# Attention over sorted edges: the destination rows held 23 times in DRAM

## The chip, the cores and the metric

The kernel runs on one core of one Trainium2 chip. The metric is the device time of one execution, in microseconds; smaller is better. TensorE (PE, with its weight loads shown apart as PEld), VectorE (DVE), ScalarE (ACT), GpSimd (POOL) and the DMA queue of SyncE (SPq) each run their own list of instructions in order and wait for one another by semaphores. DMA transfers of all queues run on the core's 16 DMA engines.

## The reference

Two graph layers over 12,500 nodes of 256 channels and 200,000 edges that are sorted by `dst`. The first is a weighted sum of neighbours. The second, where the change lies, is an attention in which node `c` attends to the sources `r` of its edges, with 8 heads of 32 channels:

```python
h = jnp.maximum(_layernorm(x, axis=-1), 0.0)
x = x + _L0_gnn_ref(h, L0_gnn_weight, edge_weight, src, dst)
h = jnp.maximum(_layernorm(x, axis=-1), 0.0)
# _L1_gnn_ref(h, edges): q, k, v = h @ W.T + b, in 8 heads; r = src, c = dst
qe = q[:, c, :]
ke = k[:, r, :]
ve = v[:, r, :]
sim = jnp.einsum('hed,hed->eh', qe, ke) * scale
m = jax.ops.segment_max(sim, c, num_segments=bs)
p = jnp.exp(sim - m[c])
s = jax.ops.segment_sum(p, c, num_segments=bs)
attn = p / s[c]
out_e = attn.T[..., None] * ve
agg = jax.ops.segment_sum(out_e, c, num_segments=bs)
return agg @ Wo.T + bo
```

## The kernel before

The program is a row of blocks that end in a barrier of all engines: the first layer (to about 3,290 us), the projections to q, k and v (to about 3,704 us), the **edge tables** (3,704 to 3,785 us), the **attention loop** (3,785 to about 6,942 us) and the output product (to 7,142 us).

**Edge tables.** 128 edges make a column, and a column that meets two blocks of 128 nodes stands once for each. There are 110 windows of 16 columns (`NW2`, `W2`), rounded up to 14 chunks of 128 columns (`C2` = 14, `R2` = 1792). For each chunk `c`, POOL gathers `fg` (src, dst and more of 128 columns), DVE forms `dlf`, the node number of each edge inside its block, ACT narrows it to bf16 as `dlb` (two buffers, `t_narrow`) and makes `brk` (marks where dst changes, two buffers), and SP stores both: `drows` (L1177) and `breaks` (L1180). ACT may write `dlb` for chunk `c` only when the store of chunk `c - 2` has landed, and likewise `brk`. ACT also copies a row `ends` (L1242). After the last chunk DVE works alone on rows made of `ends` (L1309 to L1339), and then the barrier falls. SP ends its list by waiting for the last two stores of each kind.

`drows` is one row in DRAM of `R2 * P` = 229,376 bf16 values: the node numbers of all columns, one after another.

**Attention loop.** It runs over 440 steps of 4 columns, 4 steps to a window. In a window every engine needs a one-hot matrix `OT` of 128 nodes x 16 columns x 128 edges. SP loads it as numbers: all 128 partitions get the same 16 x 128 = 2048 values (4 KB) of `drows`, 512 KB in one DMA (L1434), into one of three buffers, two windows ahead of use. DVE compares each partition with its own number (L1732), which makes the one-hot matrix. PE multiplies it with `qb`, the queries of the block (L1508, `expand`), DVE multiplies by the gathered keys and adds up per head (L1667, L1676), a chain over PE, DVE and ACT finds running maxima (L1535 to L1577, L1752 to L1799, L1628 to L1651), ACT takes the exponential and weighs the values (L1622, L1610, with a share for DVE, L1688), PE sums them per node (L1525) and DVE adds them to `acc` (L1713). POOL gathers keys and values, one indirect DMA of 128 rows of 2,080 bytes for every column (L1484), up to 11 steps ahead. SP also loads `qb` (L1412), stores finished blocks of `acc` (L1426) and loads `nf` from `breaks` (L1442). The order of all of this is written out by hand, step by step, in each engine's list.

The load, in the kernel before:

```python
e.dma_start(OT[:, w % 3, :, :].rearrange("p j e -> p (j e)"),
            drows[0:1, w * W2 * P:(w + 1) * W2 * P].to_broadcast([P, W2 * P])).then_inc(
    dls.sem(w), 16)
```

Of the kernel before, what the change touches and what calls it, by code (L numbers as in the profile page):

```python
# [7 lines left out]
P = 128  # L8
# [19 lines left out]
W2 = 16  # L28
NW2 = -(-2 * (T2 + NB - 1) // W2)
J2 = NW2 * W2  # L30
C2 = -(-J2 // P)
R2 = C2 * P
PH = NH * (W2 + 1)
BIG = 1.0e30
SCALE = float(np.float32(1.0) / np.sqrt(np.float32(32.0)))

# [3 lines left out]
BF16 = mybir.dt.bfloat16  # L40
# [50 lines left out]
def build(nc, x, src, dst, edge_weight, weight, Wq, bq, Wk, bk, Wv, bv, Wo, bo, out):  # L91
    def dram(name, shape, dt=F32):
        return nc.dram_tensor(name, shape, dt, kind="Internal").ap()

    fields = dram("fields", (JP, 3 * P))
    breaks = dram("breaks", (R2, P + 1))
    drows = dram("drows", (1, R2 * P), BF16)
    accd = dram("accd", ((NB + 1) * P, NH * 33))
    srows = dram("srows", (1, JP * P))
    sums = [dram(f"sums{k}", (NB * P + P, D)) for k in range(NS)]  # L100
# [8 lines left out]
    with ExitStack() as top:  # L109
# [3 lines left out]
        def S(name):  # L113

            if name not in known:
                known[name] = nc.alloc_semaphore(name)
            return known[name]
# [7 lines left out]
        def sb(stack, name, shape, dt=F32):  # L125
            return stack.enter_context(nc.sbuf_tensor(name, shape, dt))
# [4 lines left out]
        hw = [Landing(nc.alloc_semaphore(f"landed{i}")) for i in range(26)]  # L131
# [41 lines left out]
        with ExitStack() as stack:  # L173
# [9 lines left out]
            @block.sync  # L183
            def _(e):
                e.dma_start(da[:, :], dst.rearrange("(p e) -> p e", e=1600)).then_inc(loaded.sem(0), 16)
                e.wait_ge(S("st_fill"), 1)
                e.dma_start(db[0:124, :], dst[1:1 + 124 * 1600].rearrange("(p e) -> p e", e=1600)).then_inc(
                    loaded.sem(1), 16)
                e.dma_start(db[124:125, 0:1599], dst[1 + 124 * 1600:E].rearrange("(p e) -> p e", e=1599)).then_inc(
                    loaded.sem(2), 16)  # L190
                e.wait_ge(S("st_pad"), 3)
                edge_loads(e, src, ints[:, 0, :, :], edges[0].sem(0))
# [946 lines left out]
        with ExitStack() as stack:  # L1139
# [22 lines left out]
            bb = sb(stack, "bb", [P, R2 // 2 + 1])  # L1162
            bi = sb(stack, "bi", [P, R2 // 2], I32)
            keys, frows = Ring(hw[0:1], 2), Ring(sw[0:NF])
            dput, bput = Ring(hw[1:3]), Ring(hw[3:5])
            block = stack.enter_context(nc.Block())

            @block.sync
            def _(e):
                e.wait_ge(S("t_fill"), 1)  # L1170
                e.dma_start(kf[:, 0:6].rearrange("p (c a) -> p c a", a=1), fields[0:12 * P, P:P + 1].rearrange(
                    "(c p i) f -> p c i f", p=P, i=2)[:, :, 0, :]).then_inc(keys.sem(0), 16)
                e.dma_start(kf[0:64, 6:7], fields[12 * P:JP, P:P + 1].rearrange("(p i) f -> p i f", i=2)[:, 0, :]).then_inc(
                    keys.sem(1), 16)
                for c in range(C2):
                    e.wait_ge(S("t_narrow"), c + 1)
                    e.dma_start(drows[0:1, c * P * P:(c + 1) * P * P].rearrange("a (p f) -> (a p) f", f=P),  # L1177
                                dlb[:, c % 2, :]).then_inc(dput.sem(c), 16)
                    e.wait_ge(S("t_brk"), c + 1)
                    e.dma_start(breaks[c * P:(c + 1) * P, :], brk[:, c % 2, :]).then_inc(bput.sem(c), 16)  # L1180
                for c in range(C2 - 2, C2):
                    e.wait_ge(dput.sem(c), dput.value(c))
                    e.wait_ge(bput.sem(c), bput.value(c))

            @block.gpsimd
# [43 lines left out]
            def _(e):  # L1229
                e.wait_ge(S("t_fill"), 2)  # L1230
                for c in range(C2):
# [5 lines left out]
                    if c >= 2:  # L1237
                        e.wait_ge(bput.sem(c), bput.value(c - 2))
                    e.activation(brk[:, c % 2, 1:P], dif[:, c % 2, 0:P - 1], ACT.Copy, scale=-BIG).then_inc(
                        S("t_brk"), 1)  # L1240
# [101 lines left out]
        frows.over(C2)  # L1342
        dput.over(C2)
        bput.over(C2)


        with ExitStack() as stack:
# [12 lines left out]
            ab = sb(stack, "ab", [1, 2, NH, W2 + 1])  # L1360
            tops = sb(stack, "tops", [1, 2 * PH + 2])
            runs = sb(stack, "runs", [1, 2, PH])
            sides = sb(stack, "sides", [1, 2, NH, W2])
# [8 lines left out]
            dls, nfs, flushed = Ring(hw[8:11]), Ring(hw[11:14]), Ring(hw[14:22])  # L1372
            hs = tops[:, 0:PH]
            ts = tops[:, PH:2 * PH]
            block = stack.enter_context(nc.Block())
# [18 lines left out]
            @block.sync  # L1394
            def _(e):
                blocks, slots, news = registers(e, "l1s"), registers(e, "l1t"), registers(e, "l1u")
                fslot, fend, fblk = registers(e, "l1v"), registers(e, "l1w"), registers(e, "l1x")

                def queries(h):

                    if 4 * h >= NJ:
                        return
                    e.load(blocks[:4], irow[0:1, 4 * h:4 * h + 4])
                    own = [e.snap(r, min_val=0, max_val=NB - 1) for r in blocks[:4]]
                    e.load(slots[:4], irow[96:97, 4 * h:4 * h + 4])
                    slot = [e.snap(r, min_val=0, max_val=NQ - 1) for r in slots[:4]]
                    e.load(news[:4], irow[64:65, 4 * h:4 * h + 4])
                    new = [e.snap(r, min_val=0, max_val=1) for r in news[:4]]
                    for j in range(4 * h, 4 * h + 4):
                        if j >= NQ:  # L1410
                            e.wait_ge(S("l_expanded"), (j - NQ) // 2 + 1)
                        e.dma_start(qb[:, bass.ds(slot[j % 4], 1), :].rearrange("p a d -> p (a d)"),  # L1412
                                    qt[bass.ds(own[j % 4] * P, P), :], cond=new[j % 4],
                                    bounds_check="skip_entire_dma").then_inc(qs.sem(j), 16)

                def flush(h):

                    e.load(fslot[:4], irow[96:97, 4 * h:4 * h + 4])
                    slot = [e.snap(r, min_val=0, max_val=RB - 1) for r in fslot[:4]]
                    e.load(fend[:4], jrow[0:1, 4 * h:4 * h + 4])  # L1420
                    end = [e.snap(r, min_val=0, max_val=1) for r in fend[:4]]
                    e.load(fblk[:4], jrow[32:33, 4 * h:4 * h + 4])
                    own = [e.snap(r, min_val=0, max_val=NB) for r in fblk[:4]]
                    for j in range(4 * h, 4 * h + 4):
                        e.wait_ge(S("l_add"), j + 1)
                        e.dma_start(accd[bass.ds(own[j % 4] * P, P), :],  # L1426
                                    acc[:, bass.ds(slot[j % 4], 1), :].rearrange("p a d -> p (a d)"),
                                    cond=end[j % 4], bounds_check="skip_entire_dma").then_inc(flushed.sem(j), 16)

                def rows(w):  # L1430
                    if w < NW2:
                        if w >= 3:
                            e.wait_ge(S("l_expanded"), 4 * (w - 3) + 4)
                        e.dma_start(OT[:, w % 3, :, :].rearrange("p j e -> p (j e)"),  # L1434
                                    drows[0:1, w * W2 * P:(w + 1) * W2 * P].to_broadcast([P, W2 * P])).then_inc(
                            dls.sem(w), 16)

                def limits(w):
                    if w < NW2:
                        if w >= 3:  # L1440
                            e.wait_ge(S("l_bw2"), w - 2)
                        e.dma_start(nf[:, w % 3, :], breaks[w * W2:(w + 1) * W2, :].rearrange(  # L1442
                            "(a j) f -> a j f", a=1).to_broadcast([NH, W2, P + 1])).then_inc(nfs.sem(w), 16)

                rows(0)
                queries(0)
                rows(1)
                limits(0)
                for p in range(STEPS + 1):
                    w, u = p // 4, p % 4  # L1450
                    if u % 2 == 0:
                        queries(p // 2 + 1)
                    if u == 1:
                        rows(w + 2)
                    if u == 3:
                        limits(w + 1)
                    if u % 2 == 0 and 10 <= p < NQD + 10:
                        flush((p - 10) // 2)
                for j in range(NJ - RB, NJ):
                    e.wait_ge(flushed.sem(j), flushed.value(j))  # L1460
# [136 lines left out]
            def _(e):  # L1597
# [16 lines left out]
                for p in range(STEPS):  # L1614
# [10 lines left out]
                    if u == 1 and on:  # L1625
                        if v:
# [4 lines left out]
                        e.wait_ge(S("l_tops"), v + 1)  # L1631
                        e.copy(tops[:, :].rearrange("a (i x) -> a i x", i=2)[:, :, 0:PH].rearrange(  # L1632
                            "a i (h k) -> a i h k", h=NH)[:, :, :, 0:W2],
# [352 lines left out]
```

## Time and profile before

| | |
|---|---|
| median of 3 runs | 7138.48 us (7129.28 to 7151.11) |
| the profiled execution | 7143.95 us, its span 7142.2 us |
| edge tables | 3704 to 3785 us |
| attention loop | 3785 to 6942 us, 110 windows |
| busy share of the span | PE 64%, DVE 64%, ACT 55%, POOL 65% |
| bytes moved by DMA | 1130 MB, 158 GB/s on average |

The span runs from the first to the last instruction; 1.75 us of the profiled execution lie outside it. The busy shares are averages over blocks that are limited by different things, so they don't say what limits the block that the change touches; the rows further down are cut by stretches of time for that.

### The profile page before, as it was taken

The page shows a single profiled execution, that of the slowest core. Times are in us where ns is not written, and L with a number is a line of the kernel's source. Part 1 is how long each engine was busy: PE and PEld are TensorE (multiplying, and loading weights), DVE is VectorE, ACT ScalarE, POOL GpSimd, SP SyncE. Part 2 cuts the span into 40 slices and gives each one's busy share as a digit, 9 for nine tenths or more (in the row PEclk, how much of TensorE's full clock was granted, in tenths as well). Part 3 has the DMA queues.
Part 4 walks back from the last instruction along what each step waited for, and adds up shares of the span by engine and source line. Part 5 has one row for each costly group of instructions (what it writes and reads, how often), then busy time and mean ns, then how long its engine had stood idle before and what let it go on. Part 6 is the DMA issues. An engine that isn't in the chain of part 4 may idle for free. (4 is left out here: it accounts for less than half of the span.)

```text
span 7142.2 us, 117615 instructions
## 1 busy us (share of the span) xinstructions
PE 4603.1 (64%) x19731; PEld 3404.2 (48%) x19731; DVE 4560.8 (64%) x12314; ACT 3957.7 (55%) x14496; POOL 4635.3 (65%) x3701
## 2 busy tenths in 40 slices
PE   1466666666666666657874677677766766666767
PEld 1344444444445445544543555455544555544545
DVE  3665555555555666655655777776777776776766
ACT  0665555555555555543433666666666666666661
POOL 1578888888888888884534666566656656656530
PEclk6677777777777777778986878887888788888779
DMA  9777777777777777768845666666666666666646
GB/s 327 167 106 105 105 106 108 106 105 107 106 108 105 108 109 109 108 97 277 287 145 151 177 176 179 178 179 181 188 179 187 186 184 188 195 184 199 185 137 195
DMA packets 645045, 1130.08 MB, mean 158 GB/s; under 512 B 75393, under 2 KB 467659, under 8 KB 644309
## 3 DMA queue, kind: packets, MB, share of 16 engines
q0 software_dynamic: 367600, 678.97, 48.3%
q1 hardware_dynamic: 224849, 273.78, 11.5%
q10 hardware_dynamic: 51860, 169.74, 7.1%
q14 instruction: 546, 4.47, 0.2%
q8 instruction: 190, 3.11, 0.2%
HBM read 929.80 MB, written 451.51 MB: 193 GB/s over the span
## 5 line engine op out<-in xcount | busy, mean ns | idle before, releaser
L657 POOL DMA_INDIRECT sums<-mtw,posIw x1563 | 2489.2, 1593 | 600.2 <-issue 415.6
L1484 POOL DMA_INDIRECT kv<-kvt,sI x1760 | 1795.9, 1020 | 1201.6 <-issue 1093.5
L1610 ACT ACTIVATE pv<-kv,pp 128x33 f32<-128x33 f32 x8800 | 1915.3, 308 | 28.7 <-issue 24.8
L1525 PE MATMUL ps<-pv,Of 128*128 128x264 f32 x3520 | 1198.3, 485 | 599.1 <-DVE acc L1713 414.6
L690 PE MATMUL ps<-h,wf 128*128 x3320 | 1219.5, 522 | 310.9 <-DVE mtw L781 230.9
L674 PE MATMUL ps<-Mw,Oh 128*128 128x128 f32 x3320 | 671.2, 367 | 917.2 <-DVE Oh L808 909.5
L781 DVE SCALAR_TENSOR_TENSOR mtw<-mtw,cont,ps 128x256 f32 x1660 | 794.2, 478 | 613.1 <-SPq L646 440.3
L1525 PEld LDWEIGHTS ps<-pv,Of 128*128 128x128 f32 x3520 | 756.6, 232 | 896.8 <-issue 549.7
L674 PEld LDWEIGHTS ps<-Mw,Oh 128*128 128x128 f32 x3320 | 630.2, 274 | 1032.5 <-DVE Oh L808 993.3
L690 PEld LDWEIGHTS ps<-h,wf 128*128 128x128 f32 x3320 | 818.9, 263 | 589.4 <-issue 450.9
L755 ACT COPY wf<-ps 128x512 f32<-128x512 f32 x415 | 243.0, 586 | 1230.0 <-PE ps L674 920.8
L1508 PE MATMUL ps<-qb,OT 128*128 x5280 | 769.6, 303 | 99.5 <-issue 73.0
L1508 PEld LDWEIGHTS ps<-qb,OT 128*128 128x128 bf16 x5280 | 567.1, 109 | 283.7 <-issue 138.9
L1713 DVE SCALAR_TENSOR_TENSOR acc<-acc,keep,ps 128x264 f32 x880 | 423.0, 481 | 333.0 <-remote 239.9
L818 DVE SCALAR_TENSOR_TENSOR junk<-ints,sT,tri 128x128 f32<-128x128 f32 x1660 | 575.3, 347 | 92.2 <-issue 91.7
L836 DVE TENSOR_TENSOR posIw<-sT,step 128x1 f32 x1660 | 265.3, 160 | 476.3 <-DVE step L826 161.8
L1667 DVE TENSOR_TENSOR prod<-ps,kv 128x1024 f32<-128x1024 f32 x440 | 532.2, 1210 | 51.7 <-remote 44.0
L721 ACT ACTIVATE off<-ints,sT 128x128 f32 x1660 | 530.1, 390 | 22.3 <-issue 9.8
L732 ACT ACTIVATE Mw<-off,wT 128x128 f32<-128x128 f32 x1660 | 530.0, 389 | 13.4
L1676 DVE TENSOR_REDUCE sims<-prod 128x32 f32<-128x1024 f32 x440 | 533.8, 1213 | 0.3
L1632 ACT COPY tops<-ps 1x256 f32<-1x256 f32 x110 | 39.5, 359 | 582.8 <-remote 483.2
L726 ACT ACTIVATE off<-off,one 128x512 f32<-128x512 f32 x415 | 299.4, 722 | 13.5
(230 smaller groups left out, 4726.9 us busy)
## 6 DMA issues: line engine op xcount, KB each, us to landing
qb<-qt SPq DMA_DIRECT2D x880, 192.0 KB
accd<-acc SPq DMA_DIRECT2D x880, 132.0 KB
ints<-srows ACTq DMA_DIRECT2D x205, 512.0 KB
OT<-drows SPq DMA_DIRECT2D x110, 512.0 KB
sums<-zero ACTq DMA_DIRECT2D x72, 704.0 KB
part<-sums SPq DMA_DIRECT2D x56, 896.0 KB
kv<-kvt,sI POOLq DMA_INDIRECT x1760
kvt<-kvo SPq DMA_DIRECT2D x98, 260.0 KB
```

What stands on the lines that cost most here:

```text
L657: e.indirect_dma_start(sums[t % NS], bass.IndirectOffsetOnAxis(ap=posI[:, t % NP:t % NP + 1], axis=0), mt[:, t % NM, :], None, compute_op= ...
L674: m = e.matmul(psum[g % 2][:, j % 4 * P:j % 4 * P + P], lhsT=Oh[:, j // W % 2, j % W, :], rhs=Mw[:, j % 16, :], start=True, stop=True)
L690: m = e.matmul(psum[2 + q % 4][:, j % 2 * D:j % 2 * D + D], lhsT=BT[:, g % 3, j % 4, :], rhs=h[:, bass.ds(own[j % 4], 1), :].rearrange("p ...
L721: e.activation(off[:, 0, i, :], Sr[:, w % 3, bass.ds(row[i], 1), :].rearrange("p a b -> p (a b)"), ACT.Abs, bias=sT[:, 4 * g + i:4 * g + i ...
L781: e.scalar_tensor_tensor(out=to, in0=to, scalar=cont[:, j:j + 1], in1=psum[2 + j // 2 % 4][:, j % 2 * D:j % 2 * D + D], op0=ALU.mult, op1= ...
L818: e.scalar_tensor_tensor(out=junk[:, j % 4, :], in0=srow, scalar=sT[:, j:j + 1], in1=tri[:, :], op0=ALU.is_equal, op1=ALU.mult, accum_out= ...
L1484: e.indirect_dma_start(kv[:, s % NK, :], None, kvt, bass.IndirectOffsetOnAxis(ap=sI[:, s:s + 1], axis=0)).then_inc(kvs.sem(s), 16)
L1508: m = e.matmul(psum[Q % 2 * 2 + i // 2][:, i % 2 * D:(i % 2 + 1) * D], lhsT=OT[:, w % 3, Q % 4 * 4 + i, :], rhs=qb[:, bass.ds(slot[j % 4], ...
L1525: m = e.matmul(psum[6 + j % 2][:, 0:NH * 33], lhsT=Of[:, w % 2, k % W2, :], rhs=pv[:, k % NV, :], start=(k % 2 == 0), stop=(k % 2 == 1))
L1610: e.activation(pv[:, s % NV, h * 33:h * 33 + 33], kv[:, s % NK, D + h * 33:D + h * 33 + 33], ACT.Copy, scale=pp[:, w % 2, h, s % W2:s % W2 ...
L1667: e.tensor_tensor(prod[:, Q % 2, :, :], banks[:, Q % 2 * 2:Q % 2 * 2 + 2, :].rearrange("p b (a d) -> p (b a) d", d=D), kv[:, s:s + 4, 0:D] ...
L1676: e.tensor_reduce(sims[:, w % 2, :, Q % 4 * 4:Q % 4 * 4 + 4].rearrange("p h i -> p i h"), prod[:, Q % 2, :, :].rearrange("p a (h d) -> p a ...
```

## The change

`drows` gets 23 rows of 458,752 bytes each (`NC` = 23) in place of one. When SP has stored a chunk into row 0 and that store has landed, it copies the chunk from row 0 to rows 1 to 22 by one DMA from DRAM to DRAM, 22 rows of 16,384 bf16 values (32,768 bytes). The copy of chunk `c - 1` stands in SP's list behind the stores of chunk `c`. The wait at the end of SP's list is for the last copy, in place of the last two stores of `drows`.

The load of `OT` moves the same 512 KB. Partition `8a + b` now reads row `a + b` of `drows`, so neighbours read from different rows, and the 8 partitions of a group start one row further on than those of the group before.

```diff
+NC = 23
...
-    drows = dram("drows", (1, R2 * P), BF16)
+    drows = dram("drows", (NC, R2 * P), BF16)
...
-            dput, bput = Ring(hw[1:3]), Ring(hw[3:5])
+            dput, bput, copied = Ring(hw[1:3]), Ring(hw[3:5]), Ring(hw[5:6], C2)
...
+                def copies(c):
+
+                    cols = slice(c * P * P, (c + 1) * P * P)
+                    e.wait_ge(dput.sem(c), dput.value(c))
+                    e.dma_start(drows[1:NC, cols], drows[0:1, cols].to_broadcast([NC - 1, P * P])).then_inc(
+                        copied.sem(c), 16)
+
...
+                    if c:
+                        copies(c - 1)
+                copies(C2 - 1)
+                e.wait_ge(copied.sem(C2 - 1), copied.value(C2 - 1))
                 for c in range(C2 - 2, C2):
-                    e.wait_ge(dput.sem(c), dput.value(c))
                     e.wait_ge(bput.sem(c), bput.value(c))
...
                         e.dma_start(OT[:, w % 3, :, :].rearrange("p j e -> p (j e)"),
-                                    drows[0:1, w * W2 * P:(w + 1) * W2 * P].to_broadcast([P, W2 * P])).then_inc(
+                                    bass.AP(drows.tensor, w * W2 * P, [[R2 * P, 16], [R2 * P, 8], [1, W2 * P]])).then_inc(
                             dls.sem(w), 16)
```

SP's list in the edge tables, at the first chunks, before the change (`dlb` and `brk` are the two buffers in SBUF, `drows` and `breaks` lie in DRAM):

```order
L1177 DMA drows<-dlb 128x128
L1180 DMA breaks<-brk 128x129
L1177 DMA drows<-dlb 128x128
L1180 DMA breaks<-brk 128x129
L1177 DMA drows<-dlb 128x128
L1180 DMA breaks<-brk 128x129
```

and with the change:

```order
L1185 DMA drows<-dlb 128x128
L1188 DMA breaks<-brk 128x129
L1185 DMA drows<-dlb 128x128
L1188 DMA breaks<-brk 128x129
L1175 DMA drows<-drows 22x16384
L1185 DMA drows<-dlb 128x128
L1188 DMA breaks<-brk 128x129
L1175 DMA drows<-drows 22x16384
```

From the third chunk on, a copy stands ahead of each pair of stores on the same queue. The other engines' lists hold the same instructions as before.

## Rows read from the trace of the kernel before

**Rows 1.** Waits between 4500 and 6500 us, longest in total first.

```profile
engine line waited for: us in total, times, longest us
POOL kv L1484 <- issue: 719.9, 959, 7.4
PEld ps L1525 <- issue: 363.2, 279, 6.9
ACT tops L1632 <- remote: 324.6, 51, 8.1
PE ps L1525 <- DVE acc L1713: 271.3, 181, 6.2
```

**Rows 2.** Busy us of each engine by stretches, granted clock, DMA share, GB/s.

```profile
core 0: us, PE busy (x) PEld busy (x) DVE busy (x) ACT busy (x) POOL busy (x), PEclk, DMA share, GB/s
4000.00:4400.00 400.00, 283.61 (x1397) 205.33 (x1396) 291.32 (x473) 267.61 (x1240) 247.69 (x245) 0.80 0.62 178
...
6400.00:6800.00 400.00, 280.78 (x1386) 200.87 (x1385) 289.17 (x473) 271.52 (x1253) 242.58 (x243) 0.81 0.65 192
```

**Rows 3.** Everything that writes or reads `OT`: durations, waits before it, who waited.

```profile
L1434 SPq DMA_DIRECT2D OT<-drows x110: 3/337/713, 3785.3 to 6826.2; - x110
...
its engine sat idle before it (us, times) until:
  issue: 211.8, 192
  DMA qb<-qt: 25.1, 1
  DVE prod L1667: 1.1, 1
  DMA OT<-drows: 0.7, 1
```

**Rows 4.** Single stretches: the first within loads of `OT`, the last without one.

```profile
5110.00:5112.00 2.00, 0.07 (x1) 0.00 (x0) 0.53 (x1) 0.00 (x0) 1.42 (x2) 1.00 1.03 397
5169.00:5171.00 2.00, 1.41 (x4) 1.07 (x4) 2.00 (x4) 2.00 (x10) 1.39 (x3) 0.50 0.92 255
5220.00:5221.00 1.00, 0.53 (x5) 0.27 (x3) 1.00 (x3) 1.00 (x6) 0.69 (x2) 1.00 0.93 94
...
3552.00:3562.00 10.00, 10.00 (x40) 6.74 (x40) 5.83 (x18) 4.35 (x13) 7.14 (x7) 1.00 1.09 385
```

**Rows 5.** Timeline of SP in the edge tables, first chunks: start, duration, line.

```profile
3742.07 0.33 SPq L1177 DMA_DIRECT2D drows<-dlb  x1
3742.44 0.44 SPq L1180 DMA_DIRECT2D breaks<-brk  x1
3744.28 0.32 SPq L1177 DMA_DIRECT2D drows<-dlb  x1
3744.65 0.43 SPq L1180 DMA_DIRECT2D breaks<-brk  x1
```

**Rows 6.** The same for the last chunk and the next block.

```profile
3763.39 0.32 SPq L1177 DMA_DIRECT2D drows<-dlb  x1
3763.75 0.43 SPq L1180 DMA_DIRECT2D breaks<-brk  x1
3785.26 0.32 SPq L1434 DMA_DIRECT2D OT<-drows  x1
```

**Rows 7.** Waits of SP's list between 3741 and 3786 us.

```profile
SPq L1139 <- PEq L1139: 19.5, 1, 19.5
SPq L1180 <- ACT brk L1239: 2.8, 3, 1.1
SPq L1182 <- DMA drows<-dlb: 0.6, 1, 0.6
```

**Rows 8.** DMA by queue between 3741 and 3766 us: packets, MB, share.

```profile
q0 software_dynamic: 832, 2.56, 40.5%
q1 hardware_dynamic: 4032, 1.39, 21.8%
```

**Rows 9.** ACT and DVE at the end of the edge tables; first and last of 16.

```profile
3763.07 0.29 ACT L1235 CAST dlb<-dlf 128x128 bf16<-128x128 f32 x1
...
3764.03 2.02 DVE L1309 TENSOR_TENSOR same<-ends 1x1791 f32<-1x1791 f32 x1 [0.95 <-ACT ends L1242]
...
3784.37 0.62 DVE L1339 TENSOR_SCALAR jrow<-bi 1x896 int32<-1x896 int32 x1
```

**Rows 10.** DMA by queue from 180 to 220 us, stores of zeros to DRAM.

```profile
q10 hardware_dynamic: 2916, 10.93, 67.4%
```

**Rows 11.** DMA by queue from 4000 to 6800 us.

```profile
q0 software_dynamic: 127325, 423.84, 53.1%
q1 hardware_dynamic: 54064, 89.23, 9.7%
q8 instruction: 92, 1.51, 0.2%
```

More of the change, by code:

```diff
@@ L1344, in build @@
         bput.over(C2)
+        copied.over(C2)
         with ExitStack() as stack:
```

## The prediction

> **What bounds the kernel now.** I read the busy shares by stretches first, because the page's averages mix blocks. In the attention loop each 400 us hold 284 us of PE, 291 us of DVE, 268 us of ACT and 248 us of POOL, and the DMA engines are busy for 0.62 to 0.65 of the time [rows 2]. Nothing is full, neither an engine nor the DMA. The list of waits says why: the time goes into hand-overs. ACT waits for the maxima of a window (L1632), 324.6 us in 51 waits, PE waits for DVE's addition (L1525 behind L1713), 271.3 us in 181 waits, and POOL has gaps of 719.9 us that its gathers can afford because they run 11 steps ahead [rows 1]. So the loop is bounded by a chain between PE, DVE and ACT inside each window, and a transfer matters to it only if someone waits for it to land, or if it slows another one for which someone waits.
>
> Next I looked at who waits for the load that the change touches. Over the 110 loads of `OT` the readers waited for the load once, for 0.7 us, and that is the first load of the loop; `OT` is loaded two windows ahead, and a window lasts (6826.2 - 3785.3) / 109 = 27.9 us [rows 3]. For the other tables read in the loop the waits behind a DMA are single ones too: 25.1 us once for `qb`, at the loop's start [rows 3].
>
> **The load, read from 23 places.** Bytes, number of DMAs and destination stay. What can change is how fast DRAM gives the data, and what other transfers suffer meanwhile. In a stretch that lies inside a load of `OT`, when PE is idle and the DMA engines are full (share 1.03), they move 397 GB/s; in a stretch where partial sums are read from separate rows, they move 385 GB/s at a share of 1.09 [rows 4]. So reading one 4 KB piece 128 times can run at the engines' own rate. It doesn't always: in other loads the engines are as busy (0.92 and 0.93) and move only 255 and 94 GB/s [rows 4]. That is the part that the change could win. Were every load 1 us shorter, 110 us of time with full DMA engines would go, out of some 3,157 us in which they are busy 0.63 of the time. None of that is waited for directly, and I count the gain in the loop as nothing. Its bounds: a loss of 20 us if 23 places are read more slowly than one (the gathers, whose rows lie far apart, get 423.84 MB in 53.1% of 16 x 2,800 us, or 17.8 bytes per ns and engine, against 25.3 for the long stores of rows 10 [rows 10, 11], so at worst a load takes half as long again, some 0.6 us more, of which a third could come through), and a gain of 60 us if about half of 1 us per load comes through by way of the other queues.
>
> The Trainium skill speaks to this (DMA: Bandwidth & Descriptors, section "Latency and other measured facts"): copies whose partitions lie a large power of two apart lose rate, down to half at 4 MiB, which it guesses to be streams in step that meet in one channel of the memory. By that rule 16 engines reading one and the same 4 KB would be the worst case and a load would run at half rate, which spreading would cure; the trace's 397 GB/s says that it does not hold for all loads, the 94 and 255 GB/s leave room for it in some. It is the second rival below.
>
> **The copies.** Each of the 14 copies writes 22 rows of 32,768 bytes, 720,896 bytes, 10.1 MB in all, where the edge tables moved 2.56 + 1.39 MB in the whole stretch [rows 8]. I cost a copy by its busiest DMA engine. 22 rows don't divide among 16 engines, so some engine has at least two rows, 65,536 bytes. Between which rates? Long stores to DRAM ran at 10.93 MB in 67.4% of 16 x 40 us, or 25.3 bytes per ns and engine [rows 10]: 2.6 us per copy. The slowest long reads of DRAM in the trace are the instruction fetches, 1.51 MB in 0.2% of 16 x 2,800 us, or about 17 bytes per ns [rows 11]: 3.9 us per copy. No row shows a transfer from DRAM to DRAM.
>
> The Trainium skill (the same page, section "Why a DMA increments its semaphore by 16 and not by 1") says that a DMA runs on the largest number of engines up to 16 that divides the slowest dimension of both sides. For 22 rows that is 11 engines of two rows each. The sum would be the same by it, since the busiest engine has two rows either way.
>
> What else those engines do in a chunk: the gathers took 40.5% and SP's queue 21.8% of 25 us [rows 8], together 15.6 us over 14 chunks, 1.1 us per chunk and engine. So a chunk costs the busiest engine between 2.6 us (if the other work finds room beside the copy) and 3.7 us (if it is all added). I take 3.2 us, in the middle, because both the gathers and the stores do run on those engines but parts of a copy can overlap with them. Before, a chunk took (3763.39 - 3742.07) / 13 = 1.64 us [rows 5, 6]. The table stretch thus becomes bound by the copies, for as long as somebody waits for what is queued behind them.
>
> Who does? ACT's narrowing of chunk c waits for the store of chunk c - 2, and with the change that store stands on SP's queue behind the copy of chunk c - 4. SP itself waits for a store's landing before it issues its copy; behind this wait stand the stores of the next chunk, and behind them ACT, then DVE and PE by the buffers. A store alone lands soon: the last one was issued at 3763.39 and SP's wait for it, 0.6 us, began at 3764.2, so it took 1.4 us [rows 6, 7]. The last narrowing (chunk 13) needs the store of chunk 11, behind the copy of chunk 9, the tenth. The first copy can be issued at 3745.1, when SP has issued the second pair of stores [rows 5]. So the tenth is through at 3745.1 + 10 x 3.2 = 3777.1, the store behind it has landed at 3778.5, and from the last narrowing at 3763.07 to the first of DVE's row work at 3764.03 it is 1.0 us [rows 9]: DVE begins its rows at 3779.5 in place of 3764.0, **15.5 us later**. With 2.6 us a copy it is 3745.1 + 26 + 2.4 = 3773.5, 9.5 us later; with 3.7 us, 20.5 us; with 3.9 + 1.1 = 5.0 us, 33.5 us.
>
> The last four copies cost nothing: they lie beside DVE's rows, which take 3764.03 to 3784.99, 21.0 us [rows 9], while SP has 19.5 us of nothing to do [rows 7]. Four copies at 3.2 us and a landing are 14.2 us. That cover lasts up to (21.0 - 1.4) / 4 = 4.9 us per copy; beyond it each further us per copy costs four more. The wait that SP drops, for the last two stores of `drows`, was 0.6 us under the same cover and brings nothing. SP's 14 issues, some 0.3 us each [rows 5], fit inside the longer chunks.
>
> **The sum.** Against the profiled execution: 7143.95 + 15.5 + 0 = 7159.5 us. That execution was 5.5 us over the median of the three runs, so against the median it is 7138.5 + 15.5 = 7154 us, 0.2% more. I put the forecast at 7153.
>
> **The rivals.**
>
> *The copies are dear (slower).* One mechanism: each copy holds two rows on one engine for more than 2.6 us, as it reads and writes DRAM at the rate of the instruction fetches, and all stores behind it land that much later. At 5.0 us a chunk the price is 33.5 us: 7172 us. It decides from about 3.8 us per chunk, where 10 x 3.8 - 16.5 makes 21.5 us, the 0.3% of the median. For it: no row shows a copy inside DRAM, 3.8 is just over the upper end of my range with the better rate, and were fewer than 11 engines used (two, say), it would be many times that. Against: stores of the same size run at full rate, and 32 KB pieces are long.
>
> *The loop gets faster.* The loads that move 94 or 255 GB/s with busy engines [rows 4] become like the one with 397, and the gathers and loads of `qb` beside them move on, which shortens some of the waits of the chain. With half of 1 us in each of 110 windows: -55 + 15.5, 7099 us. For it: those two stretches. Against: nobody waits for `OT` [rows 3], and with a share of 0.63 the DMA has room to catch up.
>
> *Nothing is seen.* The copies run beside the gathers and the stores overtake them, because different queues or free engines carry them; the loop stays: 7138 to 7144 us. Against it: copies and stores are on one queue.
>
> *The loop gets slower* because rows in 23 places cost DRAM more than one that was just read: up to +20 in the loop, with the copies 7174 us. Against: the gathers' rows are smaller and random.
>
> **How the numbers follow.** A measurement of this kernel can tell about 0.3%, 21 us, from no change. The forecast, +8 to +20 us, has 0.38; the copies dear 0.25; nothing seen (under +8) 0.14; the loop faster 0.15; the loop slower 0.08. So faster by over 0.3% has 0.15 less a little, for gains that don't cover the copies: 0.14. Slower by over 0.3% has 0.25 + 0.08, and 0.01 from the upper edge of the forecast: 0.34. The rest, 0.52, is within 0.3%. For 8 times in 10 the range must take in the forecast, nothing seen, and most of the dear copies, and part of the small gains: 7125 to 7183 us.
>
> **What would show it.** In the profile after: a group of 14 DMAs `drows<-drows` on SP's queue, 10.1 MB more on it; the stores in the edge tables 2.6 to 3.7 us apart in place of 1.64; DVE's first row work (L1309 before) 10 to 20 us later and still 21 us long; no wait of SP for the last copy that lasts beyond DVE's rows. In the loop: windows of 27.9 us as before, the busy shares of rows 2 unchanged, still no wait for `OT`. Wrong would be: stores of `drows` still 1.6 us apart (copies hidden), over 3.8 us apart (copies dear), or a loop from the first to the last load of `OT` that is more than 15 us shorter or longer than 3040.9 us [rows 3], beyond what executions differ by.

## The result, and the profile after

The changed kernel took 7170.15 us in the median of 7 runs (7149.78 to 7184.66), the kernel before, timed beside it, 7138.93 us (7129.28 to 7151.93). The ratio is 1.0039, with a 95% interval from 1.0026 to 1.0052: the change makes the kernel 0.39% slower, just over what a measurement can tell from no change. The profiled execution took 7171.29 us, 27.3 us over that of before; its span is 7169.5 us.

I cut the two spans at the same events and compared the pieces:

| stretch | before | after | difference |
|---|---|---|---|
| start to the first store of `drows` | 3742.1 | 3737.3 | -4.8 |
| first store to DVE's first row work | 22.0 | 44.7 | +22.7 |
| DVE's row work, to the first load of `OT` | 21.2 | 21.2 | 0.0 |
| first to last load of `OT` | 3040.9 | 3054.3 | +13.4 |
| last load of `OT` to the end | 315.9 | 312.0 | -3.9 |

The first and the last row hold no changed work; they show by how much two executions differ anyway. The edge tables stand out. The timeline of SP there (start, duration, line, what the DMA moves), at its beginning and its end:

```profile
3737.26 0.33 SPq L1185 DMA_DIRECT2D drows<-dlb  x1
...
3740.32 0.86 SPq L1175 DMA_DIRECT2D drows<-drows  x1
...
3742.32 0.75 SPq L1175 DMA_DIRECT2D drows<-drows  x1
...
3767.74 0.74 SPq L1175 DMA_DIRECT2D drows<-drows  x1
...
3774.36 0.74 SPq L1175 DMA_DIRECT2D drows<-drows  x1
...
3781.78 0.49 SPq L1185 DMA_DIRECT2D drows<-dlb  x1
...
3784.43 3.74 SPq L1175 DMA_DIRECT2D drows<-drows  x2
```

The stores of `drows` are (3781.78 - 3737.26) / 13 = 3.42 us apart, for the 1.64 us that [rows 5, 6] give. The copy at 3767.74 is the eighth, that at 3774.36 the tenth, and the last row begins with the thirteenth. ACT's narrowings in the same stretch, the last two, and DVE's rows, the first and the last, which answer to [rows 9]:

```profile
3778.08 0.30 ACT L1246 CAST dlb<-dlf 128x128 bf16<-128x128 f32 x1 [2.62 <-DMA drows<-dlb]
...
3781.05 0.30 ACT L1246 CAST dlb<-dlf 128x128 bf16<-128x128 f32 x1 [2.09 <-DMA drows<-dlb]
```

```profile
3781.95 2.01 DVE L1320 TENSOR_TENSOR same<-ends 1x1791 f32<-1x1791 f32 x1 [5.99 <-ACT ends L1253]
...
3802.30 0.62 DVE L1350 TENSOR_SCALAR jrow<-bi 1x896 int32<-1x896 int32 x1
```

Ten of the fourteen narrowings now wait for a store to land, 27.9 us in all, where one waited, for 0.6 us, before, and DVE's rows wait 5.99 us for ACT where they waited 0.95 us. The rows themselves take 20.97 us as before. The waits of ACT behind the stores, in the list of its waits between 3741 and 3830 us:

```profile
ACT dlb L1246 <- DMA drows<-dlb: 27.9, 10, 3.8
```

The waits of SP's list between 3741 and 3830 us (total, times, longest), against [rows 7]:

```profile
SPq L1175 <- DMA drows<-dlb: 21.8, 11, 3.9
SPq L1140 <- PEq L1140: 10.1, 1, 10.1
SPq L1140 <- DMA drows<-drows: 4.6, 1, 4.6
```

SP waits 21.8 us in 11 waits for the landing of a store before it may copy it. At the end it waits 4.6 us for the last copy and then still 10.1 us for the barrier, so the last copies hold nobody. The DMA of the stretch from 3741 to 3800 us by queue (packets, MB, share), against [rows 8], and its new group of issues:

```profile
q1 hardware_dynamic: 3962, 11.30, 55.5%
q0 software_dynamic: 640, 1.97, 11.3%
...
drows<-drows SPq DMA_DIRECT2D x14, 704.0 KB
```

In the loop the load of `OT` (durations, first and last start; then what its readers waited for), against [rows 3]:

```profile
L1446 SPq DMA_DIRECT2D OT<-drows x110: 3/452/1002, 3803.2 to 6857.5; - x110
...
  DMA qb<-qt: 24.7, 1
  DMA OT<-drows: 2.0, 1
```

It is waited for once, by 2.0 us in place of 0.7 us. The two stretches of [rows 2] (busy us of PE, PEld, DVE, ACT, POOL, clock, DMA share, GB/s):

```profile
4000.00:4400.00 400.00, 277.47 (x1376) 200.24 (x1374) 286.25 (x467) 265.66 (x1229) 239.43 (x241) 0.81 0.63 175
6400.00:6800.00 400.00, 282.00 (x1382) 202.57 (x1382) 285.28 (x466) 266.29 (x1233) 239.56 (x241) 0.81 0.66 189
```

and the two waits of [rows 1] that carry the chain:

```profile
ACT tops L1644 <- remote: 321.8, 52, 8.3
...
PE ps L1537 <- DVE acc L1725: 251.1, 182, 5.8
```

In the loop no engine waits for something new. One thing did change: SP's queue keeps the DMA engines busy for more of the time while it moves no more bytes. Between 4000 and 6800 us, against [rows 11]:

```profile
q0 software_dynamic: 126444, 420.93, 53.3%
q1 hardware_dynamic: 53208, 87.98, 11.2%
```

9.7% before, 11.2% now. In the trace's records of single transfers, the 4 KB pieces of `OT` take 231 ns in the median, 159 ns before. The loads became slower to move by being read from 23 places, or so it seemed.

### The profile page after: what moved, and what is told of

Same layout as the page of the kernel before. It is cut to its first block and busy times, and to the rows that moved or that the text cites. A ratio compares the mean times of both kernels' runs of the same rounds, so it can differ in the third digit from the quotient of the medians.

```text
span 7169.5 us, 117628 instructions
## 1 busy us (share of the span) xinstructions
PE 4617.6 (64%) x19731; PEld 3412.7 (48%) x19731; DVE 4559.5 (64%) x12314; ACT 3958.7 (55%) x14496; POOL 4625.2 (65%) x3701
## 5 line engine op out<-in xcount | busy, mean ns | idle before, releaser
L1622 ACT ACTIVATE pv<-kv,pp 128x33 f32<-128x33 f32 x8800 | 1915.1, 308 | 32.0 <-issue 27.8
L733 ACT ACTIVATE Mw<-off,wT 128x128 f32<-128x128 f32 x1660 | 530.0, 390 | 13.4
```

The source lines that it names most:

```text
L1622: e.activation(pv[:, s % NV, h * 33:h * 33 + 33], kv[:, s % NK, D + h * 33:D + h * 33 + 33], ACT.Copy, scale=pp[:, w % 2, h, s % W2:s % W2 ...
```

## The experiments

Two questions were open. Do the copies alone account for the result, and by which of their properties? And why are the pieces of `OT` slower, and does that cost anything? Kernels that ran on one chip are compared with the kernel before on that chip: the chips differ by more than the change does (medians of before: 7180.76, 7152.02 and 7134.77 us).

### The two halves of the change, each alone

The copies alone: the 23 rows are written, and the load reads row 0 as before.

```diff
-                                    bass.AP(drows.tensor, w * W2 * P, [[R2 * P, 16], [R2 * P, 8], [1, W2 * P]])).then_inc(
+                                    drows[0:1, w * W2 * P:(w + 1) * W2 * P].to_broadcast([P, W2 * P])).then_inc(
```

> The 14 copies are made as in the changed kernel, but the load of OT reads row 0 by the broadcast as before; the copied rows are read by nobody. Theory A (both parts cost: the copies delay the edge tables, and 23 places are read more slowly than one): the edge tables, from the first store of drows to the first of DVE's row work, take 44.7 us as in the changed kernel, not 22.0 as before; SP's queue takes 9.7% of the DMA engines' time from 4000 to 6800 us as before, not 11.2%; the time is 20 to 25 us over before (ratio about 1.003), 5 to 12 us under the changed kernel. Theory B (only the copies cost): the same tables, but the time equals the changed kernel's, 29 to 33 us over before, and the loop is as long as there.

The form alone: the kernel before, its load from row 0 written with two outer steps of zero, as the changed load has two.

```diff
-                                    drows[0:1, w * W2 * P:(w + 1) * W2 * P].to_broadcast([P, W2 * P])).then_inc(
+                                    bass.AP(drows.tensor, w * W2 * P, [[0, 16], [0, 8], [1, W2 * P]])).then_inc(
```

> The kernel before with one edit: the load of OT is written as 16 x 8 pieces with both steps 0, so the form of the DMA is that of the changed kernel and the place read is one row; no copies. Theory A (places matter, not the form): SP's queue stays at 9.7% of the DMA engines' time from 4000 to 6800 us, first load waited for 0.7 us, time within 0.15% of before. Rival C (the three-dimensional form itself makes the pieces slow): 11.2%, first load waited for about 2 us, time up to 12 us over before.

Measured: the copies alone 7213.07 us, ratio 1.0041 (1.0028 to 1.0054); the form alone 7210.18 us, ratio 1.0042 (1.0027 to 1.0056). The whole time with the copies alone is that of its theory B, 32 us over before; the share of the loading queue, below, is that of its theory A. The copies carry the change in the tables. DVE's first row work with the copies alone, whose first store of `drows` is at 3741.54:

```profile
3788.63 2.01 DVE L1320 TENSOR_TENSOR same<-ends 1x1791 f32<-1x1791 f32 x1 [6.88 <-ACT ends L1253]
```

47.1 us from store to rows; with the form alone it is 23.3 us. The shares of SP's queue in the loop (4000 to 6800 us), first with the copies alone, then with the form alone:

```profile
q1 hardware_dynamic: 52352, 86.73, 9.5%
```

```profile
q1 hardware_dynamic: 52573, 86.97, 10.8%
```

So the slower pieces (159 and 219 ns) come with the form, though the form alone reads one and the same row. The 23 places aren't what moves the median. But the whole time of the form alone, 29 us over before, was a surprise: with the copies' 32 us it would make some 60 us, and the changed kernel was only 31 us over its own kernel before. The two don't add up, so both ran again below.

### The rows further apart, and the copies at the end

In one kernel a row got 4 KB more (`RP = R2 * P + 2048`), so that the places are 462,848 bytes apart for 458,752, all else as changed.

```diff
-    drows = dram("drows", (NC, R2 * P), BF16)
+    drows = dram("drows", (NC, RP), BF16)
...
-                                    bass.AP(drows.tensor, w * W2 * P, [[R2 * P, 16], [R2 * P, 8], [1, W2 * P]])).then_inc(
+                                    bass.AP(drows.tensor, w * W2 * P, [[RP, 16], [RP, 8], [1, W2 * P]])).then_inc(
```

> The changed kernel with each row of drows 4 KiB longer (462,848 bytes apart in place of 458,752). Theory A1 (the distance, 7 x 64 KiB, makes the 16 engines meet in the same part of DRAM): SP's share of DMA time falls from 11.2% back to about 9.7%, and the time falls by up to 10 us under the changed kernel. Theory A2 (any set of many places is slower than one): the share stays at 11.2% and the time that of the changed kernel within 0.1%. The edge tables take 44.7 us by both.

Measured: 7227.34 us, ratio 1.0064 (1.0051 to 1.0078); rows of DVE 48.0 us after the first store, pieces of 236 ns. The distance of the rows does not matter to the pieces. The whole time, 47 us over before, fits neither theory: both had it at the changed kernel's or under. (The Trainium skill, DMA: Bandwidth & Descriptors, section "Latency and other measured facts", ties a loss to pitches that are large powers of two. No run here tests that: rows 458,752 bytes (7 x 65,536) or 462,848 bytes apart are not a power of two apart, and partitions that share one row, to which the prediction stretched it, have no distance at all.)

In the other all fourteen copies stand behind the last store, all else as changed.

```diff
-                    if c:
-                        copies(c - 1)
-                copies(C2 - 1)
+                for c in range(C2):
+                    copies(c)
```

> The changed kernel, but SP issues all 14 copies behind the last store, so that no store stands behind a copy. The copies need 14 x 3.3 us on the busiest engines or, without gathers and stores beside them, 14 x 2.5 to 2.6 = 36 us. Theory A (the stores behind the copies are what delays the tables): DVE's row work begins 22 us after the first store, as before, and lasts 21 us; the copies end 36 to 38 us after the last store, 15 to 17 us after DVE's rows, so the barrier falls 15 to 17 us later than before and 5 to 8 us sooner than in the changed kernel; the time is 24 us or so over before where the changed one is 31 over. Rival D (the copies slow the gathers by sheer load of the DMA engines, whatever their order): DVE's row work begins over 30 us after the first store even so.

Measured: 7215.62 us, ratio 1.0052 (1.0036 to 1.0068). DVE's rows start where they did before, and SP then waits for the copies. The first store is at 3741.98. DVE's first row work, SP's waits between 3740 and 3805 us; and the DMA from 3775 to 3800 us, where the copies have the DMA almost to themselves:

```profile
3765.40 2.01 DVE L1319 TENSOR_TENSOR same<-ends 1x1791 f32<-1x1791 f32 x1 [1.17 <-ACT ends L1252]
```

```profile
SPq L1140 <- DMA drows<-drows: 26.5, 1, 26.5
...
SPq L1140 <- PEq L1140: 0.2, 1, 0.2
```

```profile
q1 hardware_dynamic: 332, 7.24, 67.5%
```

This is the cleanest reading of how the copies delay the rows. The store at which ACT waits was held up by the copies ahead of it on its queue: with them gone the rows come 23.4 us after the first store. The price moves to the end: the barrier waits for the last copy, and the first load of `OT` comes 61.4 us after the first store, for 43.2 in the kernel before and 65.9 in the changed one. And it gives the price of a copy by itself: its pieces of 32,768 bytes take 1.21 us, two of them one after the other on an engine, and the copies follow each other every 2.43 us. Against the kernel before the tables thus cost some 18 us here, but the whole time was 35 us over before, where theory A had 24; the other 17 us are not explained by these rows. (The load has the 16 by 8 form, and on this chip the form alone had been 29 us over before.) A share of 67.5% is that of 11 of 16 engines (68.8%). By the Trainium skill (DMA: Bandwidth & Descriptors, section "Why a DMA increments its semaphore by 16 and not by 1") 22 rows run on 11 engines; the trace agrees.

### Places without the form, and another form

Before and the changed kernel ran again on a second chip, beside two more. One has the copies and reads 128 different places, 79,360 bytes apart over all 23 rows, in the plain form with one outer step. It reads numbers of other columns, so `OT` holds other edges.

```diff
-                                    bass.AP(drows.tensor, w * W2 * P, [[R2 * P, 16], [R2 * P, 8], [1, W2 * P]])).then_inc(
+                                    bass.AP(drows.tensor, w * W2 * P, [[39680, P], [1, W2 * P]])).then_inc(
```

The other is the kernel before with two outer steps of 64 and 2.

```diff
-                                    drows[0:1, w * W2 * P:(w + 1) * W2 * P].to_broadcast([P, W2 * P])).then_inc(
+                                    bass.AP(drows.tensor, w * W2 * P, [[0, 64], [0, 2], [1, W2 * P]])).then_inc(
```

> The kernel before once more, as a comparison with itself, to have its trace from the same chip as the runs beside it and to see what the comparison can tell. By every theory: ratio 1 within 0.15%; SP's queue 9.7% of the DMA engines' time from 4000 to 6800 us.

> The changed kernel again, beside the others. If copies (22 to 25 us) and the form of the load (15 to 29 us) add up, it is 40 to 50 us over before (ratio 1.006 to 1.007), like the variant with rows 4 KiB longer on the earlier chip. If the first measurement (1.0039) holds, the form costs less here than it did alone, and 28 us come out, ratio 1.004.

> The changed kernel with its copies, but partition p reads 4 KB at p x 79,360 bytes, written as 128 pieces with one step: the two-dimensional form of before, 128 different places over the same 10 MB. The numbers read are those of other columns, so the attention's result is another one; the amount of work and of bytes is the same. Theory C' (the form makes the load slow, not the places): SP's share from 4000 to 6800 us back to 9.7%, first data of the load 1.0 us after its issue as before instead of 1.4, and the time that of copies alone, 22 to 32 us over before. Theory A2 (many places are slower): share 11%, time 5 to 20 us over copies alone. Rival (spreading helps once the form doesn't hinder): 10 us or more under copies alone.

> The kernel before with the load written as 64 x 2 pieces, both steps 0: one place, no copies, three-dimensional form again, split elsewhere. If the number of dimensions makes the load slow: SP's share 10.8% or so and 15 to 29 us over before, like 16 x 8. If it is the 16 as outer count (that each of the 16 engines' parts begins a new outer piece): 9.7% and no difference from before.

| kernel | us | ratio (95%) | store to DVE's rows | pieces of `OT` |
|---|---|---|---|---|
| before again | 7149.24 | 1.0002 (0.9988 to 1.0017) | 22.6 us | 159 ns |
| changed again | 7182.28 | 1.0041 (1.0024 to 1.0059) | 47.8 us | 231 ns |
| 128 places, plain form | 7174.37 | 1.0029 (1.0017 to 1.0041) | 45.0 us | 159 ns |
| 64 by 2, row 0 | 7157.15 | 1.0009 (0.9997 to 1.0022) | 22.7 us | 159 ns |

SP's queue in the loop, 4000 to 6800 us, with 128 places in the plain form, and then with 64 by 2:

```profile
q1 hardware_dynamic: 52928, 87.72, 9.7%
```

```profile
q1 hardware_dynamic: 54064, 89.23, 9.6%
```

Reading from 128 places in 10 MB of DRAM has the same median piece and the same share as reading one row 128 times. It is not quite as fast: over the 14,080 pieces of the loop, 6.4% take over 0.4 us, where the eight executions that read one row, in whatever form, have 3.3 to 4.1% and the six that read 23 or 128 places 5.9 to 6.6%. The mean is 199 ns, for 188 to 194 from one row in one step (all from the records of transfers). In the whole time none of this can be seen: the ratio, 1.0029, is no higher than those of the copies alone, 1.0041 and 1.0033. The loss of 20 us that I allowed for and the gain of the rival "the loop gets faster" did not come; a few us either way lie inside the intervals. What lengthens the median piece is the 16 by 8 form; two outer steps of 64 and 2 don't. Both two-step forms delay the first data of the loop's first load (1.38 us after the issue for 0.96 us, as worked out from the records of the transfers). Why 16 by 8 gives longer pieces stays open.

### The halves again, and a smaller copy

On a third chip the form alone, the copies alone and the changed kernel ran side by side, and with them the copies into 16 rows in place of 22, load from row 0.

```diff
-NC = 23
+NC = 17
```

> The kernel before, with the load of OT from row 0 as before but written as a source of 16 by 8 by 12,800 elements (both outer steps zero): the form of the changed load alone, a second time. A, the form costs time in the loop: ratio 1.004, some 29 us over before, of which the stretch from the first to the last load of OT holds some 10 to 15 us. B, the form only makes the load's pieces last longer, for which nobody waits, and the first such run read high: ratio 1.000 within 0.0015. Both: tables as before, first store of drows to first row work 22 to 24 us; share of the loading queue in the loop 10.8%.

> The fourteen copies alone, the load as before from row 0, a second time. A: the tables carry the change, 22 to 26 us, ratio 1.0033. B: something in the loop comes on top of the copies, ratio over 1.0045. Both: first store of drows to first row work 44.5 to 48 us; share of the loading queue in the loop 9.5%.

> The changed kernel beside its two halves. A, the form costs 20 to 30 us: it stands 20 us or more over the copies alone, ratio 1.007. B, only the copies cost: it stands within 8 us of the copies alone, ratio 1.0035 to 1.0045.

> Copies into 16 further rows in place of 22 (17 rows in all), the load as before from row 0. A, a copy's time follows the rows that each of the engines at work has to write, two of them with 22 rows and one with 16: the stores of drows come some 1.3 us closer (2.0 to 2.3 us apart for 3.4), and the row work begins at 22 to 32 us after the first store, for 44.7. B, it follows the bytes in all, by 16 to 22: stores 2.5 to 2.9 us apart, row work some 35 to 39 us after the first store. C, it is a fixed cost of each copy: 3.2 to 3.5 us apart, row work at 43 us or more. The whole time follows: ratio 1.0000 to 1.0012 in A, 1.002 in B, 1.0035 in C.

| kernel | us | ratio (95%) | store to DVE's rows | first to last load of `OT` |
|---|---|---|---|---|
| form alone | 7146.62 | 1.0010 (0.9999 to 1.0022) | 22.8 us | 3033.1 us |
| copies alone | 7163.71 | 1.0033 (1.0020 to 1.0046) | 46.8 us | 3041.6 us |
| changed | 7166.59 | 1.0038 (1.0025 to 1.0051) | 44.2 us | 3054.6 us |
| 16 rows copied | 7156.05 | 1.0020 (1.0008 to 1.0033) | 36.9 us | 3054.2 us |

The changed kernel stands 2.9 us over the copies alone, and the copies alone 29 us over before: the copies are nearly all of it, as B had it. The form alone gave 12 us here where it had given 29 us; its ratio, 1.0010, is inside what B allows and far from A's 1.004. (The recorded ratios, which are not those of the medians, make it 24 us for the copies alone and 7 us for the form.) The last column shows why the loop can't be read from single executions: the copies alone and the 16 rows have the same loop and the same load, and differ by 12.6 us in it.

With 16 rows the stores are 2.80 us apart, the first and the last at

```profile
3740.24 0.33 SPq L1185 DMA_DIRECT2D drows<-dlb  x1
...
3776.69 0.58 SPq L1185 DMA_DIRECT2D drows<-dlb  x1
```

and DVE's rows start at

```profile
3777.13 2.01 DVE L1320 TENSOR_TENSOR same<-ends 1x1791 f32<-1x1791 f32 x1 [5.30 <-ACT ends L1253]
```

36.9 us after the first store, between the 22.7 us without copies (mean of five executions) and the 46.2 us with 22 rows (mean of seven). (36.9 - 22.7) / (46.2 - 22.7) = 0.60 of the cost, for 16 / 22 = 0.73 of the bytes and for half of the rows on the busiest engine. All three numbers that theory B forecast came: 2.80 us, 36.9 us, ratio 1.0020 (whose interval leaves room for the others). Theory A, by which only the rows on the busiest engine count, had the rows at 32 us or earlier, and theory C, a fixed cost of each copy, at 43 us or more; both are out.

That the bytes are the cause isn't shown even so. The last of the fourteen copies has no gather and no store beside it. From first data to last end it took 1.73 us with 16 rows, and 2.99 to 3.42 us with 22 rows in the seven executions that have them between the stores (all from the records of transfers). So a copy by itself goes with the rows on the busiest engine, as theory A says. It is the sequence of copies and stores that doesn't: with 16 rows the copies were still issued 2.80 us apart after the last gather was done. A rival that no run tests is the order in SP's list. SP issues a copy only when a store has landed that stands behind the copy before the last one; it waits 18.9 us in 12 such waits with 16 rows. The kernel with all copies last takes away the gathers, the stores and these waits together, so it doesn't tell them apart.

## Why the prediction was right in its place and small in its size

**The bound, and nobody waits for `OT`: right.** The chain of waits in the loop is the same, and the load is waited for once, 2.0 us in place of 0.7 us. A transfer that got 45% longer per piece costs little because it is issued two windows ahead.

**The load from 23 places, counted as nothing: right about the places, within what can be seen.** 128 places read like one in the median; the tail of slow pieces that they add, 6.4% for 3.3 to 4.1%, is not seen in the time. Slower pieces in the median did come, by the form in which the source is written, which the prediction had not priced at all. What that costs, five pairs on one chip each tell: 2.9 us (changed over copies alone), 7.9 us (changed over 128 places in the plain form), 14.3 us (rows further apart over copies alone), 11.9 and 29.4 us (form alone over before). All have the same sign, but each is a difference of two medians that are known to some 9 us. The ratios to before say less: the changed kernel has 1.0039, 1.0041 and 1.0038, the copies without the form 1.0041, 1.0033 and 1.0029, and the difference of the means is 0.0005, or 3.6 us. So the form costs some us, more likely under 15 than over, and neither its size nor its place in the loop is settled.

**The copies, and whom they hold: right mechanism, term too small.** The tables' rows came 22.7 us later, for 15.5 predicted. The order is as told: ten copies, the store behind the tenth, the last narrowing, the rows. From the records of the transfers, against the terms of the sum:

- The first copy was issued 3.06 us after the first store (3740.32 - 3737.26); the prediction had 3.03.
- From its issue to its first data it took 2.07 us (1.6 to 2.4 us in the other kernels with copies), which the sum left out: it let the tenth copy end ten copy times after the first one's issue.
- Ten copies, from first data to the last end, took 37.2 us, 3.72 us each, where the sum had 3.2. This is the term that was mis-sized. The mean is that of "all added", 2.6 + 1.1 = 3.7, but that it meets it so well is partly luck. The 1.1 us holds gathers and stores, and the last gather's data ended at 3767.2, while the seventh copy ran. Up to there the copies' first data lay 3.9 us apart, and from there to the last copy 3.25 us (their issues, from 3767.74 to 3784.43, 3.34 us), with no gather left and only some 0.36 us of stores per chunk and engine beside the 2.43 us of a copy with only copies around it (all from the records of transfers). Some 0.5 us per copy is unexplained; the waits of SP between copies are a candidate that no run tests.
- From the tenth copy's end at 3779.60 to the last narrowing at 3781.05 it is 1.45 us (predicted 1.4), and from there to the rows 0.9 us (1.0).

2.07 + 10 x 0.52, and small differences in the other terms, make 7.2 us, the whole gap between 22.7 and 15.5.

**The last four copies beside DVE's rows: right.** SP was done 10.1 us before the barrier fell. The kernel with all copies last shows the other side: fourteen copies don't fit under 21 us of rows, and then SP's wait for them sets the barrier.

**The sum and the side.** 7153 us was forecast and 7170 measured, inside the range. The loss was twice what was forecast, 31 us by the medians and 28 us by the ratio for 15, and outside the +8 to +20 us that the forecast had set itself. I held a change within 0.3% for likelier than a loss over 0.3%; it came out at 0.39%, slower. The rival "the copies are dear" decides from 3.8 us a chunk, and 3.72 us is just short of that; but the latency of 2.07 us, which stood in neither, put the tables at 22.7 us, over its 21.5. The other 5 us of the measured 27.8 (0.39% of 7139) are the form's, or noise. With two terms out by 7 us the outcome crossed a bound that the forecast had approached to 6 us.

**The other rivals.** "Nothing is seen" is wrong: the stores stand behind the copies, 3.42 us apart. "The loop gets faster" is wrong: with 128 places in the plain form the slow pieces of a load became more, not fewer, so the two stretches with few GB/s at busy engines [rows 4] can't be put down to reading one place. "The loop gets slower" had the sign of the pieces right, a mean of 199 ns for 188 to 194, and nothing of it is seen in the time; the few us that are open lie with the form as far as is known.

## What to carry to other kernels

Spreading the source of a broadcast load over DRAM bought nothing here, where most pieces already came at the engines' rate (4096 bytes in 159 ns), and it is worth less than nothing if the copies have to be made in a stretch where a queue is waited for: look at who waits for what stands behind a new DMA on its queue. Cost a large DMA in a queue by its busiest engine's bytes plus all the other work of those engines, plus the time from its issue to its first data once for the chain, and take the sum rather than a middle, as a lower estimate: it gave 2.43 + 1.1 = 3.5 us for the 3.72 us of 22 rows, but 1.2 + 1.1 = 2.3 us for the 3.0 us of 16 rows (30.4 us from the first data of the first copy to the end of the tenth). A term of some 20 us in 7,100 can't be found in the loop's span of one execution; it can in a stretch of 40 us cut at fixed events.

## What the runs showed of the hardware beyond that

- A copy inside DRAM of 22 rows of 32 KB kept 67.5% of 16 engines busy, as 11 of them would: 32,768 bytes in 1.21 us, 27 bytes per ns and engine, no slower than the long stores of [rows 10]. With nothing between them they come every 2.43 us. Where stores had stood between the copies, the last copy, with nothing beside it, took 2.99 to 3.42 us, and with 16 rows 1.73 us.
- The same 128 pieces of 4 KB take 159 ns in the median when the source is written as 128, or as 64 by 2, and 219 to 236 ns when it is written as 16 by 8, whether the steps are zero or 448 KB (seven executions with the form, seven without). Both forms with two outer steps had their first data 0.4 us later.
- Reading one row 128 times or 128 places once made no difference to the median piece, 159 ns, or to the share, 9.5 to 9.7% of the loop. The slow tail grew: 5.9 to 6.6% of the pieces took over 0.4 us from 23 or 128 places (six executions), 3.3 to 4.1% from one row (eight executions), in either form.
